# Decoder with two layers on one core: in layer 0's attention the next tile's scores are issued ahead of the output projection, VectorE adds the attention's result between the two halves of the shifts, and two smaller steps move with them

## The reference, cut to what matters

```python
def reference(x, ctx_2048, mask_BxS2_bk0, ...):          # x: 16 sequences of 64 tokens, 256 channels
    x = x + _L0_attn_ref(_layernorm(x), Wq, Wk, Wv, Wo)   # 16 heads of 16, rotary, causal softmax
    x = x + _L0_xattn_ref(_layernorm(x), ctx_2048, mask)  # one head, reads out of ctx, masked softmax
    x = x + _L0_ffn_ref(_layernorm(x), ...)               # 8 experts, 2 of them for a token, and 2 shared ones
    x = x + _L1_attn_ref(_layernorm(x), ...)
    x = x + _L1_xattn_ref(_layernorm(x), ctx_2048, ctx_2048)
    x = x + _L1_ffn_ref(_layernorm(x), ...)               # 16 experts, 4 of them for a token
    return x

def _layernorm(x, eps=1e-05):
    m, v = mean(x), var(x)
    return (x - m) / sqrt(v + eps)
```

## Time and profile before

| | |
|---|---|
| median of 3 runs | 847.58 us (844.66 to 853.8) |
| the profiled execution | 854.5 us, of which span 852.7 us |
| busy over the span | PE 89%, DVE 73%, ACT 54%, POOL 28% |
| granted TensorE clock, mean | 0.958 of full |
| layer 0's attention | from the start to about 135 us |

### The profile page before, as it was taken

How to read it: one execution, slowest core, us unless ns; L and a number is a source line. 1 busy time by engine, 2 the same in 40 slices (tenths; PEclk the granted TensorE clock), 3 DMA queues, 4 the chain that set the end, 5 groups by cost and what they waited for, 6 DMA issues and landing times. The chain is left out here.

```text
span 852.7 us, 15058 instructions
## 1 busy us (share of the span) xinstructions
PE 762.7 (89%) x4897; PEld 541.9 (64%) x4897; DVE 622.5 (73%) x1364; ACT 462.9 (54%) x1012; POOL 239.2 (28%) x296
## 2 busy tenths in 40 slices
PE   6888878999998999998689989889989878999995
PEld 2455555888787887883236555555555537888884
DVE  3699955544676776753987999999996457888854
ACT  2366634334475776650324766666565407888860
POOL 2244420340000000004641423544531421333340
PEclk8799979999999999999987999999999898999999
DMA  9454551281499999926600001011125119999817
GB/s 337 179 203 196 221 198 37 93 323 42 154 316 358 342 343 416 328 91 170 202 25 1 25 7 49 25 49 34 46 77 216 56 54 345 410 410 398 325 57 253
DMA packets 57105, 158.01 MB, mean 185 GB/s; under 512 B 7180, under 2 KB 36748, under 8 KB 51708
## 3 DMA queue, kind: packets, MB, share of 16 engines
q1 hardware_dynamic: 51700, 141.97, 45.7%
q0 software_dynamic: 5328, 15.08, 4.9%
HBM read 114.21 MB, written 42.81 MB: 184 GB/s over the span
## 5 line engine op out<-in xcount | busy, mean ns | idle before, releaser
L2173 ACT ACTIVATE b_PX<-ps 128x512 f32<-128x512 f32 x128 | 72.7, 597 | 44.3 <-PE ps L2408 42.4
L1906 DVE TENSOR_REDUCE b_smax<-ps 128x4 f32<-128x1024 f32 x64 | 77.7, 1214 | 13.4 <-PE ps L2384 13.3
L1368 PE MATMUL ps<-f_rd,f_rhT 128*128 128x256 f32 x230 | 63.5, 391 | 5.1 <-issue 4.3
L2701 POOL DMA_INDIRECT y<-f_ys,f_to x47 | 45.1, 959 | 81.5 <-DVE f_to L2779 78.0
L2408 PE MATMUL ps<-b_Q,b_Cx 100*128 100x256 f32 x256 | 54.9, 321 | 6.0 <-ACT b_PX L2173 5.8
L1678 POOL MEMSET b_half<- 128x1 f32 x1 | 0.1, 98 | 205.2 <-POOLq L69 205.2
L2408 PEld LDWEIGHTS ps<-b_Q,b_Cx 100*128 100x128 f32 x256 | 40.8, 200 | 26.5 <-issue 11.5
L2384 PE MATMUL ps<-b_Cx,b_Q 96*128 96x512 f32 x128 | 46.7, 448 | 8.5 <-ACT b_Q L2157 5.1
L998 ACT ACTIVATE f_gate<-ps 128x256 f32<-128x256 f32 (+1 forms) x69 | 24.1, 349 | 50.9 <-PE ps L1280 50.7
L1182 DVE TENSOR_TENSOR f_rwl<-f_rg,f_rwh 128x1024 fp32r<-128x1024 f32 (+1 forms) x36 | 37.6, 1045 | 13.0 <-ACT f_rwh L1008 13.0
L1368 PEld LDWEIGHTS ps<-f_rd,f_rhT 128*128 128x128 f32 x230 | 38.8, 193 | 12.0 <-issue 5.7
(11 more groups left out here) (352 smaller groups left out, 2225.2 us busy)
## 6 DMA issues: line engine op xcount, KB each, us to landing
f_rg<-w_routed SPq DMA_DIRECT2D x23, 1280.0 KB, 8.4
rows<-a_blank SPq DMA_DIRECT2D x16, 1152.0 KB, 6.9
f_rd<-w_routed SPq DMA_DIRECT2D x23, 640.0 KB, 5.6
f_rw<-w_ffn SPq DMA_DIRECT2D x19, 704.0 KB, 7.5
rw<-w_ffn SPq DMA_DIRECT2D x16, 704.0 KB, 7.7
later<-w_ffn SPq DMA_DIRECT2D x12, 704.0 KB, 7.9
f_xs<-rows SPq DMA_DIRECT2D x31, 144.0 KB, 6.6
f_yk<-y SPq DMA_DIRECT2D x8, 512.0 KB, 8.5
```

Source lines behind the costliest of these rows:

```text
L1368: mm = nc.tensor.matmul(ps[:, 7, 0:D], rhT[u % 3][:, c, :], rd[b % R_SLOTS][:, off:off + D], start=(i == 0 and c == 0), stop=(i == PER - 1 ...
L1906: nc.vector.tensor_reduce(smax[t % 2][:, k // C, k % C, :], ps[:, FIRST:FIRST + 2, :].rearrange("p u (g n) -> p (u g) n", g=2), AX, ALU.ma ...
L2173: nc.scalar.activation(PX[g % RING][:].rearrange("p c m -> p (c m)"), ps[:, RETS + G_TURN[g] % 2, :], ACT.Exp, scale=XSC).then_inc(turn_re ...
L2701: pool.indirect_dma_start(y_dram, bass.IndirectOffsetOnAxis(ap=to[b % A_SLOTS][:, 0:1], axis=0), ys[b % Y_SLOTS][:], None).then_inc(y_sent ...
```

## The change

Four steps move, all in `attention0`:

- On TensorE `score` is no longer the first step of a round, for `a_`, but stands ahead of `project_out(a_)`, for `e_`: the same scores, issued in the round before, ahead of the output projection and of the transposes of the first norm.
- On VectorE `add_attention(b_)` stands between `shift(a_, 0)` and `shift(a_, 1)` instead of ahead of both.
- On VectorE `low_part(c_)` is the last step of the round instead of standing between `x_shift` and `x_probs`.
- The addition of eps in each layer norm goes from VectorE (with the wait ahead of it) to GpSimd (with a wait behind it).

The lists of ScalarE and SyncE are as they were.

```diff
@@ -311,6 +311,8 @@
                     return
                 s = t % 2
                 pool.wait_ge(var_ready[k], t + 1)
+                step.done(nc.gpsimd.tensor_scalar(veps[k][s][:], mv[k][s][:, 1:2], EPS, None, ALU.add))
+                step.wait()
                 step.done(nc.gpsimd.tensor_tensor(rstd[k][s][:], veps[k][s][:], half[:, 0:1], ALU.pow))
                 step.wait()
                 nc.gpsimd.tensor_scalar(shift_by[k][s][:], mv[k][s][:, 0:1], rstd[k][s][:], -1.0, ALU.mult, ALU.mult
@@ -362,9 +364,7 @@
                 s = t % 2
                 step.done(nc.vector.bn_stats(stats[k][s][:], X[:, t, :]))
                 step.wait()
-                step.done(nc.vector.bn_aggr(mv[k][s][:], stats[k][s][:]))
-                step.wait()
-                nc.vector.tensor_scalar(veps[k][s][:], mv[k][s][:, 1:2], EPS, None, ALU.add).then_inc(var_ready[k], 1)
+                nc.vector.bn_aggr(mv[k][s][:], stats[k][s][:]).then_inc(var_ready[k], 1)
@@ -466,20 +466,20 @@
             for n in SPAN:
                 f_, e_, a_, b_, c_ = tiles(n)
+                shift(a_, 0)
                 add_attention(b_)
-                shift(a_, 0)
                 shift(a_, 1)
                 row_sums(a_, 0)
                 row_sums(a_, 1)
                 rope(e_)
                 x_shift(b_)
-                low_part(c_)
                 x_probs(b_)
                 take(f_)
                 if f_ == 0:
                     set_masks()
                 place_k(e_)
                 add_read_out(b_)
+                low_part(c_)
@@ -745,7 +745,6 @@
             for n in SPAN:
                 f_, e_, a_, b_, c_ = tiles(n)
-                score(a_)
                 if e_ == 0:
                     keep_busy(1)
                 project(e_)
@@ -765,6 +764,7 @@
                 x_read_out(b_)
                 if b_ == TILES - 1:
                     keep_busy(10)
+                score(e_)
                 project_out(a_)
                 turn_xn(f_, 0)
                 if a_ == TILES - 1:
```

## The result

The changed kernel took 858.44 us in the median of six runs (851.62 to 861.29), the kernel before 848.78 (844.66 to 853.8): a ratio of 1.0095 with a 95% interval of 1.0062 to 1.0128, so some 8 us slower, 5.3 to 10.9. (The ratio is not that of the two medians, which alone would give 9.7 us.) Nine more runs beside 26 of the kernel before, on another occasion, gave 1.0096 (1.0058 to 1.0134). The forecast was 5.9 us slower, 853.5 us. The profiled execution took 857.88 us with a span of 856.1, where the one before had 854.5 and 852.7: 3.4 us more, less than half of what the timed runs say. So there are two things to explain, the loss and this gap.

A forecast was written before the change was run, and what follows sets the result against it. VectorE was full, but TensorE's scores ended just before each shift, so the chain M to T and back bounds: -1.54 + 6.03 + 1.05 + 0.36 = +5.9, 847.6 to 853.5 us; own range 850.5 to 856.5, whole range 847.5 to 859.

The forecast's parts named there:

- five rounds: Rounds 0 to 5 of layer 0's attention: 13.16 us each for 12.01, five take 65.80 for 59.77, a loss of 6.03.
- last tiles: End of the stage: first shift 0.97 us earlier, ScalarE's copy of the turned norms 2.02 later, net loss 1.05.
- first tiles: Start of the stage: T of round -1 stays at 30.09, T of round 0 at 43.05 for 44.59, gain 1.54 us.
- From T to M: T, start of TensorE's L641, to M, start of the round's first shift (L408): 3.85 us for 5.04, gain 1.19.
- From M to T: First shift to next L641: norm ahead of ScalarE's exponentials delays VectorE's row sums 2.34 us, 1.33 of it waiting; T is M + 9.31.
- two norms behind it: Second and third norm of the last tile, in one chain: each costs 0.18 us more, 0.36 together.
- faster side: Rival, ScalarE's exponentials not held by the norm: row sums at M + 3.66, rounds 11.83, whole 844.5 us; chance 0.09.
- L464 did not stay long: Rival, VectorE's low_part stays at 1.25 us, held by GpSimd's small norm instructions: 0.70 a round, whole 857.0; chance 0.08.
- The clock in the full rounds: Rival, TensorE falls to half clock in the full rounds: 2 us a round, whole 864 us; chance 0.05.

The follow-up runs named there:

- o_low: The kernel before with only low_part moved to the end of VectorE's round: ratio 0.9983 to the kernel before.
- u_hold: The changed kernel with ScalarE's apply_norm(b_, 1) behind both exponentials instead of ahead of them: ratio 1.0036 to the kernel before.
- mix: The changed kernel with apply_norm(b_, 1) between ScalarE's two exponentials and VectorE's take ahead of x_probs: ratio 1.0017 to the kernel before.
- low_warm: The kernel before with low_part last and seven blank matmuls in two idle stretches of TensorE at the first tiles: ratio 0.9981 to the kernel before.
- o_eps: The kernel before with only the addition of eps moved from VectorE to GpSimd: ratio 1.0019 to the kernel before.

## Where the prediction was right and where it was wrong

The mechanism was right and the size short: 5.9 us for 8.0 (5.3 to 10.9). The median is 4.9 above the 853.5 and outside the forecast's own range of 850.5 to 856.5, though inside the whole range; 1.2 of the 4.9 is the kernel before, whose median rose to 848.78 with three more runs. That the difference came so near is in part luck: the five rounds and the last tiles cost 0.9 and 1.4 us less than foretold, the first tiles up to 3.5 more. Point by point:

- **From T to M.** Foretold 3.85, measured 3.72. The scores were 0.13 earlier, since the probabilities of the cross-attention no longer wait behind L464: L722 stands at T + 1.32 instead of 1.63. L464 at 0.39 was as foretold, and the rule that the prediction took from the Trainium skill, SBUF — State Buffer, terms, held; o_low shows the same (0.41 to 0.42) with nothing else changed.
- **From M to T.** Foretold 9.31, measured 9.27. The addition of eps took 0.23 and the next instruction came 0.31 behind it, for 0.36. The row sums start at M + 4.94, foretold 4.99, with 1.22 us of waiting, foretold 1.33. That the cause is the norm's place in ScalarE's list is shown by u_hold, which moves nothing else; mix agrees.
- **Five rounds.** T of round 0 to T of round 5 took 108.65 - 43.72 = 64.93, a loss of 5.16 where I had 6.03. In the other profile of the changed kernel it took 67.48, since one of the rounds had the low clock in it (below).
- **Last tiles: a term that was not there.** M of the last full tile follows T by 3.72 instead of 4.82, and L730 follows M by 5.73 instead of 3.71: a net loss of 0.92, foretold 1.05. The two norms behind it cost 0.22 each, foretold 0.18. But from T of round 5 to L1186 the two profiles of before have 31.88 and 31.84, and the two of the changed kernel 32.03 and 31.79: nothing is left of the 1.41 that I had. L716 and what follows it ran at the low clock in both profiles of before and at the full clock in both of the changed kernel (L716 took 0.48 in both, then 0.33 and 0.34), and I had no term for it. The first profile of each:

```profile
117.47 0.48 PE L716 MATMUL ps<-K,a_xp 128*128 128x128 f32 x1 [0.80 <-DVE a_xp L449]
...
122.59 0.33 PE L716 MATMUL ps<-K,a_xp 128*128 128x128 f32 x1 [0.81 <-DVE a_xp L449]
```

Whether this gain belongs to the new order is open: o_low and low_warm, with one order there, show 0.33 and 0.47.
- **First tiles: the term that failed.** I wrote of a gain of 1.54, 33.74 + 9.31 = 43.05 against 44.59. Two things were wrong. First, the 44.59 was no fair measure. I had read in the rows that TensorE's clock was low there and treated the fall as a feature of the kernel before that the change might remove; but it comes in some executions and not in others. Where it does not come, the kernel before has T of round 0 at 41.80. Second, "T of round -1 is 30.09 and stays" was wrong. From T of round -2 (17.68 in the changed kernel) it follows by 13.05 and 13.04 us in the two changed profiles and by 12.46 in both of before. In the new order the first norm's turn stands behind the scores, so the projection of tile 1 starts 1.2 us later, runs at half clock for 3.78 us (2.21 and 2.81 before), and the turns queue behind it without a gap until L641 at 30.73. I had let that work fill the idle stretch; it ran over it. From T of round -2 to T of round 0 it is 26.04 and 26.03 us now and was 26.96 and 24.05: a gain of 0.9 or a loss of 2.0, by whether the fall comes in the kernel before. TensorE in the changed kernel:

```profile
24.22 3.78 PE L616 MATMUL ps<-a_W,a_xT 128*128 128x512 f32 x4 [0.46 <-ACT a_xT L506]
27.93 1.86 PE L625 MATMUL ps<-a_W,a_xT 128*64 128x128 f32 x16
29.72 1.09 PE L672 MATMUL ps<-K,a_e 128*128 128x128 f32 x8
30.73 0.66 PE L641 MATMUL ps<-K,a_qk 128*128 128x128 f32 x4
```

The clock had been low through L616 and L625 and had risen by the time of L641 (0.66). In the other profile of the changed kernel it fell one round later: L641 at 43.05 took 1.12, and the next followed 15.53 us behind it instead of 12.99. The idle stretches ahead of that place were the same in both profiles (0.46, 0.60, 0.60 and 0.34 us). So the end of the stage is 140.7 or 142.3 in the changed kernel and 136.2 or 133.4 in the kernel before. The differences run from 4.4 to 8.9, and the pair that I had first was at the low end. That, and 1.0 us behind the stage, is most of the gap between 3.4 and 8. The mean of the differences is 6.7, within the interval of the timed runs; the remaining 1.3 us is not explained, and with two profiles of each I can't say more of how often each case comes.

- **The rivals.** The exponentials are held, so the faster side fell, with rounds of 12.99 instead of 11.83. L464 did not stay long. The clock in the full rounds did not fall in the profiles of the changed kernel after round 0, but it did with add_attention alone, at about the price per round that I had given that rival (2 us; measured 1.0 to 2.4). There an idle stretch of 1.34 came ahead of the fall; but in o_eps one of 1.38 had no fall behind it, so the length that the rival went by does not decide alone.

## What to carry to other kernels

In a pipeline whose engines each have a fixed list, an instruction may be moved only together with what stands ahead of its users: here add_attention moved on VectorE, while the norm that needs it kept its place ahead of the exponentials on ScalarE, and the 2.3 us by which the row sums come later were readable from the rows of three engines before anything ran. Issuing something earlier on an engine that is nearly full makes what it overtakes later, and moves that look harmless or harmful alone (14.17 and 13.59 a round) can come out quite differently together (12.99). Before a term is worked out against a profiled stretch in which TensorE's granted clock is low, ask whether another execution of the same kernel shows it too: a foretold gain of 1.54 was a gain of 0.9 or a loss of 2.0, by which execution one takes.

## What the runs showed of the hardware

- A subtraction with both inputs in SBUF (L464, 128x256) takes 1.12 to 1.26 us on VectorE where GpSimd's addition of 128x512 has begun ahead of it, and 0.39 to 0.43 elsewhere, with one of 0.54 in o_eps beside the end of GpSimd's multiplication of 128x512. In all 31 such cases it ended 0.27 to 0.29 us after GpSimd's instruction. The other way round, where L464 had begun first, GpSimd's small instruction was the longer one: its addition of eps 0.29 to 0.30 us instead of 0.23, its power in o_low 0.65 to 0.66 instead of 0.55. The prediction rested on the first half; in o_low nothing else was changed on VectorE, and all of its L464 took 0.41 to 0.42.
- TensorE's granted clock around 30 us is not a property of the kernel. In six profiles with the same order on TensorE up to there it was at 1.2 GHz in three and at 2.4 GHz in three, and where it fell the stage ended later by 2.8 us in the pair that can be compared.
- What follows the first stage is the same code in all kernels of this study, and it took between 709.2 and 716.6 us, 715.4 and 709.2 in two executions of the changed kernel. So the spans of two single profiles can lie some 6 us apart without any part of the stage in it.
